# The first of four causal-attention chunks computed with its keys down the partitions, as the other three are

## The reference

```python
xn = layernorm(x)                                   # eps 1e-5
# attention on xn
x_norm = layernorm(xn) * gamma + beta
q, k, v = x_norm @ qkv[:, :512], x_norm @ qkv[:, 512:1024], x_norm @ qkv[:, 1024:]
scores = where(causal, (q @ k.T) / sqrt(512), -inf)
attn = softmax(scores) @ v @ o_proj + xn
# feed-forward on xn
h = silu(xn @ w_gate) * (xn @ w_up)                 # 2048 x 2048
h = the two of each group of 4 that are largest by magnitude, the others 0
return x + attn + h @ w_down
```

## Time and profile before

| | |
|---|---|
| median of 3 runs | 789.93 us (789.58 to 789.95) |
| the profiled execution | 789.84 us |
| its span, first to last instruction | 788.0 us |
| PE busy | 783.7 us, 99% of the span, 3518 matmuls |
| DVE busy | 610.8 us, 78% |
| ACT busy | 318.9 us, 40% |
| POOL busy | 16.7 us, 2% |
| DMA | 121.74 MB, mean 154 GB/s |

### The profile page before, as it was taken

One profiled execution on the slowest core, in us unless ns is written; L12 is line 12 of the kernel. 1 busy time (PEld: TensorE's weight loads), 2 busy tenths in 40 slices (PEclk: granted clock), 3 DMA queues, 4 the chain that ended last, 5 costly groups with the idle time before them and its releaser, 6 DMA issues.

```text
span 788.0 us, 9292 instructions
## 1 busy us (share of the span) xinstructions
PE 783.7 (99%) x3518; PEld 649.1 (82%) x3518; DVE 610.8 (78%) x964; ACT 318.9 (40%) x514; POOL 16.7 (2%) x26
## 2 busy tenths in 40 slices
PE   9999999999999999999999999999999999999998
PEld 6888878888888888888888888888888888888887
DVE  6988788678535797789989789798658658659786
ACT  5432250235123473464643634463423424335431
POOL 2011110010000000000000000000000000000000
PEclk9999999999999999999999999999999999999999
DMA  9541704500121643684454352697277163161002
GB/s 317 190 161 55 241 0 163 192 20 1 54 94 40 214 172 122 199 343 179 187 211 181 143 189 106 269 355 284 79 280 260 48 240 126 62 240 54 0 1 107
DMA packets 31611, 121.74 MB, mean 154 GB/s; under 512 B 3088, under 2 KB 3664, under 8 KB 29136
## 3 DMA queue, kind: packets, MB, share of 16 engines
q1 hardware_dynamic: 30272, 119.00, 40.9%
q10 hardware_dynamic: 1296, 2.16, 0.9%
HBM read 77.07 MB, written 44.07 MB: 154 GB/s over the span
## 4 chain that ended last, share of the span: by engine, by line
PE 98%; DMA 1%; SPq 0%; ACT 0%; DVE 0%; issue 0%
PE bank L960 13%; PE bank L958 13%; PE bank L959 13%; PE bank L701 10%; PE bank L699 10%; PE bank L700 10%; PE bank L1038 7%; PE bank L838 7%; PE bank L1040 7%; PE bank L1039 7%; DMA raw<-L_attn_qkv 1%; SPq L483 0%; PE bank L709 0%; PE bank L804 0%; PE bank L771 0%; PE bank L1051 0%
## 5 line engine op out<-in xcount | busy, mean ns | idle before, releaser
L958 PE MATMUL bank<-X_hi,wset 128*128 128x512 f32 x448 | 174.6, 390 | 0.0
L959 PE MATMUL bank<-X_lo,wset 128*128 128x512 f32 x448 | 174.5, 389 | 0.0
L960 PE MATMUL bank<-X_hi,wset 128*128 128x512 f32 x448 | 174.5, 389 | 0.0
L960 PEld LDWEIGHTS bank<-X_hi,wset 128*128 128x128 f32 x448 | 84.1, 188 | 17.5
L959 PEld LDWEIGHTS bank<-X_lo,wset 128*128 128x128 f32 x448 | 84.1, 188 | 17.5
L958 PEld LDWEIGHTS bank<-X_hi,wset 128*128 128x128 f32 x448 | 84.1, 188 | 17.3 <-issue 0.2
L1038 PE MATMUL bank<-dw,hs_hi 128*128 128x512 f32 x224 | 87.3, 390 | 0.0
L1039 PE MATMUL bank<-dw,hs_hi 128*128 128x512 f32 x224 | 87.2, 389 | 0.0
L1040 PE MATMUL bank<-dw,hs_lo 128*128 128x512 f32 x224 | 87.2, 389 | 0.0
L1672 DVE TENSOR_TENSOR acc<-bank,acc 128x512 f32<-128x512 f32 x59 | 40.2, 688 | 40.0 <-PE bank L1040 39.6
L699 PE MATMUL bank<-zg,xT 128*128 128x512 f32 (+2 forms) x132 | 49.9, 378 | 0.0
(11 more groups left out here) (259 smaller groups left out, 1445.3 us busy)
## 6 DMA issues: line engine op xcount, KB each, us to landing
w_operands<-wset SPq DMA_DIRECT2D x8, 3584.0 KB, 13.2
wset<-w_operands SPq DMA_DIRECT2D x8, 3584.0 KB, 12.2
wsum<-w_units SPq DMA_DIRECT2D x28, 256.0 KB, 3.4
dw_raw<-L_ffn_w_down SPq DMA_DIRECT2D x14, 512.0 KB, 5.0
xw<-L_attn_x SPq DMA_DIRECT2D x4, 1024.0 KB, 9.9
xt_raw<-x_t SPq DMA_DIRECT2D x8, 512.0 KB, 9.2
xn_t<-xt_raw SPq DMA_DIRECT2D x8, 512.0 KB, 2.8
acc<-resid SPq DMA_DIRECT2D x2, 2048.0 KB, 10.1
```

The source lines that it names most:

```text
L958: pe.matmul(dst[:], u[:, 0, :], x_hi, start=(first and kt == 0), stop=False, skip_group_check=True)
L959: pe.matmul(dst[:], u[:, 0, :], x_lo, start=False, stop=False, skip_group_check=True)
L960: last = pe.matmul(dst[:], u[:, 1, :], x_hi, start=False, stop=(kt == 1), skip_group_check=True)
```

## The change

Chunk 0 is made wide too: `WIDE = range(NCH)`. The kinds `scores`, `exp`, `head` and `attend` and the ring of transposed exponentials go. Chunk 0 has four units, all on the diagonal, and three parts for the softmax: unit 0, unit 1, units 2 and 3 together. Its maximum goes into one tile instead of a pair (no `max_fold`), its sums too (`first_sums`). The stretch between the products z(0) and the second chunk is written anew; all row steps of chunk 0 come into the stretch of chunk 1, and their stores and loads go to SP's queue; `row_turn(2)` comes behind the first unit of chunk 1. Units go round the banks from where the products stand (`unit_bank`), and the transposes of statistics for chunks 2 and 3 take bank 2 (`row_bank`). The matrix `causal` for the other orientation is no longer made.

```diff
-    steps += [*vo, *stat[1][0:2], *z[0], *stat[1][2:4], x_stats[1], x_rstd[1], xw_load[3], v[0][0],
-              ("scores", 0, 0), exp[0], x_scale[1], row_copy[1], v[0][1], row_turn[1], row_store[1], row_spread[1]]
-    before = {3: [z_round[1][0]]}
-    between = {3: [*stat[2][2:4], x_stats[2], x_rstd[2], *z_round[1][1:4], *z[1], x_scale[2]]}
-    beside = {0: [*stat[2][0:2], v[0][2]],
-              1: [xh_pre[1][0], v[0][3], xh[1][0]],
-              2: [xh_pre[1][1], xh_pre[1][2], xh[1][1], xh_pre[1][3], xh[1][2], xh[1][3]]}
-
-    WIDE = (1, 2, 3)
-    OLD = TC * WIDE[0]
-    for i in range(OLD):
-        steps += before.get(i, [])
-        steps.append(("head", i, 0))
-        if i >= 1:
-            steps.append(("rows_store", i - 1, 0))
-        steps += between.get(i, [])
-        if i + 1 < OLD:
-            steps += [("scores", i + 1, 0), exp[i + 1]]
-        steps += [*beside.get(i, []), ("attend", i, 0), ("rows", i, 0), ("rows_load", i + 1, 0)]
+
+    WIDE = range(NCH)
 
     def wide_units(c):
...
+    u = unit[0]
+    steps += [v[0][0], *u[0:2], x_scale[1], *u[2:4], ("max_all", 0, 0), row_turn[1], row_copy[1], row_store[1], row_spread[1], v[0][1]]
+    steps += softmax(0, {1: [v[0][2]], 2: [v[0][3]]}, {})
+    steps += [xh_pre[1][0], *meet[0][0:2]]
+    steps += [step for k in range(KT) for step in (*xh_pre[1][k + 1:k + 2], xh[1][k], z_round[1][k])]
+    steps += [*stat[2], x_stats[2], x_rstd[2], meet[0][2], *z[1], x_scale[2], ("sum_turn", 0, 0)]
     u = unit[1]
-    steps += [row_turn[2], row_copy[2], row_store[2], row_spread[2], *u[0:2], ("rows_store", OLD - 1, 0), *xn[1], xt_load[2], xn_store[1],
-              *stat[3], x_stats[3], x_rstd[3], xt_load[3], *u[2:4], x_scale[3], u[4], row_turn[3], row_copy[3], row_store[3], xh_pre[2][0], u[5],
-              xh_pre[2][1], xh[2][0], u[6], xh_pre[2][2], xh[2][1], u[7], ("max_fold", 1, 0), ("max_all", 1, 0), ("rows_load", OLD + 1, 0),
+    steps += [u[0], row_turn[2], row_copy[2], row_store[2], *rows_of[0][0], *rows_of[0][1], row_spread[2], ("rows_load", 2, 0), ("rows_load", 3, 0),
+              u[1], *xn[1], xt_load[2], xn_store[1], *stat[3], x_stats[3], x_rstd[3], xt_load[3], *rows_of[0][2], *rows_of[0][3],
+              ("rows_load", 4, 0), ("rows_load", 5, 0), *u[2:4], x_scale[3], u[4], row_turn[3], row_copy[3], row_store[3], xh_pre[2][0], u[5],
+              xh_pre[2][1], xh[2][0], u[6], xh_pre[2][2], xh[2][1], u[7], ("max_fold", 1, 0), ("max_all", 1, 0),
               xh_pre[2][3], xh[2][2], v[1][0], xh[2][3], *v[1][1:4], *z_round[2]]
     steps += softmax(1, {}, {2: [*z[2], *xn[0], xn_store[0]], 4: [("block_sum", 0, 0)]})
-    steps += [("sum_turn", 1, 0), row_spread[3], *rows_of[1][0], *rows_of[1][1], ("rows_load", OLD + 2, 0), ("rows_load", OLD + 3, 0)]
+    steps += [("sum_turn", 1, 0), row_spread[3], *rows_of[1][0], *rows_of[1][1], ("rows_load", 6, 0), ("rows_load", 7, 0)]
...
-                elif kind == "rows_store" and n >= OLD:
+                elif kind == "rows_store":
                     sp.wait_ge(rows_ready, n + 1)
                     sp.dma_start(resid_dram[n], row_slot(n)).then_inc(resid_stored[n % 2], 16)
-                elif kind == "rows_load" and OLD + 2 <= n < NT - 2:
+                elif kind == "rows_load" and n < NT - 2:
                     load_rows(n)
...
-            nc.gpsimd.memset(causal[:], 0.0).then_inc(pool_step, 1)
...
-            def score_product(n, g):
-                t, count = score_spans(n)[g]
-                no, a = prod_no["scores", n, g], n % TC * P
-                if n == 0:
...
-                if no >= TURN_RING:
-                    pe.wait_ge(turn_free, no - TURN_RING + 1)
-                row_bank_free(no)
+                if n == 1:
+                    pe.wait_ge(prod_free, 2 * KT)
+                elif n == 3:
+                    pe.wait_ge(wide_kept, units_ahead[1] + LENT_BANK + 1)
                 pe.wait_ge(scale_ready, n + 1)
...
-            def turn_probs(n, g):
-                no = turn_no["probs", n, g]
...
-                for b, t in enumerate(key_tiles(n)[g]):
-                    last = pe.transpose(dst_bank[:, b * P:(b + 1) * P], raw[:, n % 2, t * P:(t + 1) * P], ident[:])
-                last.then_inc(turn_full, 1)
...
-                    pe.wait_ge(prod_free, prods_before[c])
-                    if c > WIDE[0] and u == SUM_BANK:
-                        pe.wait_ge(sums_read, c - WIDE[0])
+                    pe.wait_ge(prod_free, max(prod_no["z", c, KT - 1] + 1, prods_before[c] - PROD_RING + u + 1))
+                    if c > 0 and u == SUM_BANK:
+                        pe.wait_ge(sums_read, c)
                 else:
                     pe.wait_ge(wide_kept, seen + u - PROD_RING + 1)
+                if c == 1 and u % PROD_RING == LENT_BANK:
+                    pe.wait_ge(turn_free, 2 + u // PROD_RING)
...
                 for m in range(KT):
                     if n == WIDE[-1] and q == 0:
                         pe.wait_ge(wide_kept, units_ahead[n] - PROD_RING + 1 + m)
+                    elif n == 1 and q == m == 0:
+                        pe.wait_ge(wide_kept, units_ahead[n])
...
                 elif kind == "v":
                     pe.wait_ge(prod_free, prod_no["vo_weight", 0, KT - 1] + 1)
                     pe.wait_ge(xh_ready, KT * (n + 1))
-                    if n in (WIDE[0], WIDE[-1]):
+                    if n == 0 and k:
+                        pe.wait_ge(wide_kept, k)
+                    elif n in (1, WIDE[-1]):
                         pe.wait_ge(wide_kept, units_ahead[n] + len(wide_units(n)) - PROD_RING + 1 + k)
                     product(kind, n, k, (xT_hi[n], xT_lo[n]), k * P, (vo_hi, vo_lo))
-                elif kind == "scores":
-                    pe.wait_ge(prod_free, prod_no["z", n // TC, KT - 1] + 1)
-                    for g in range(len(score_spans(n))):
-                        score_product(n, g)
-                elif kind == "head":
-                    turn_head(n)
-...
                 masked = step(nc.vector.tensor_tensor(block[:, 0:P], block[:, 0:P], causal_t[:], ALU.add))
                 dve.wait_ge(vec_step, masked)
-                wide_done[c] = step(nc.vector.tensor_tensor(half[:, u % 2, a:W], half[:, u % 2, a:W], block, ALU.max))
+                if c:
+                    wide_done[c] = step(nc.vector.tensor_tensor(half[:, u % 2, a:W], half[:, u % 2, a:W], block, ALU.max))
+                    return
+                one = max_one[0][:, a:W]
+                if u == 0:
+                    wide_done[c] = step(nc.vector.tensor_copy(one, block))
+                    return
+                dve.wait_ge(vec_step, wide_done[c])
+                largest_yet = nc.vector.tensor_tensor(one, one, block, ALU.max)
+                if u < TC - 1:
+                    wide_done[c] = step(largest_yet)
+                else:
+                    largest_yet.then_inc(max_folded, 1)
 
...
+            def first_sums(j):
+
+                dve.wait_ge(exp_made, j + 1)
+                whole = sum_pair[0][:, 0, :]
+                if j == 0:
+                    sums_done[0] = step(nc.vector.tensor_copy(whole, raw_part(0, 0)))
+                    return
+                for u in wide_parts(0)[j]:
+                    some = whole[:, unit_cols(0, u):W]
+                    dve.wait_ge(vec_step, sums_done[0])
+                    added_up = nc.vector.tensor_tensor(some, some, raw_unit(0, u), ALU.add)
+                    if u < TC - 1:
+                        sums_done[0] = step(added_up)
+                    else:
+                        added_up.then_inc(sums_ready, 1)
+
             def add_part(c, j):
 
                 sums, units = sum_pair[c], wide_parts(c)[j]
+                if c == 0:
+                    first_sums(j)
+                    return
                 dve.wait_ge(exp_made, parts_ahead[c] + j + 1)
                 if j < 2:
```

More of the change, by code:

```diff
@@ L67, in attention_ffn @@
     xn = [fills("xn", c)[0:2] for c in range(NCH)]
-    exp = [("exp", n, 0) for n in range(NT)]
     hi, lo = ([fills(kind, m) for m in range(4)] for kind in ("split_hi", "split_lo"))
@@ L134, in attention_ffn @@
     steps += softmax(2, {-1: [z[3][2]], 0: [z[3][3]], 1: v[2][0:2], 2: v[2][2:4]}, {4: [xn[3][0]], 5: [xn[3][1], xn_store[3]]})
-    steps += [("sum_turn", 2, 0), *rows_of[2][0], ("rows_load", OLD + 6, 0), *rows_of[2][1], ("rows_load", OLD + 7, 0)]
+    steps += [("sum_turn", 2, 0), *rows_of[2][0], ("rows_load", 10, 0), *rows_of[2][1], ("rows_load", 11, 0)]
     u = unit[3]
@@ L140, in attention_ffn @@
     w_hi_steps, w_lo_steps = fills("w_hi", 0), fills("w_lo", 0)
-    steps += [*u[0:4], *rows_of[2][2], ("rows_load", OLD + 8, 0), *rows_of[2][3], ("rows_load", OLD + 9, 0), *u[4:6], ("w_sum", 0, 0), u[6],
+    steps += [*u[0:4], *rows_of[2][2], ("rows_load", 12, 0), *rows_of[2][3], ("rows_load", 13, 0), *u[4:6], ("w_sum", 0, 0), u[6],
               *w_hi_steps[0:2], *u[7:9], *w_lo_steps[0:2], *u[9:], ("max_fold", 3, 0),
@@ L147, in attention_ffn @@
```

(36 more changed lines are left out.)

150 lines of the change are left out of this document (34 added, 116 removed).

## The result

| | before | after |
|---|---|---|
| median | 789.75 us (789.55 to 789.95, 4 runs) | 795.54 us (795.19 to 796.23, 4 runs) |
| the profiled execution | 789.84 us | 795.4 us |
| its span | 788.0 us | 793.4 us |

What follows compares the result with a forecast made beforehand. TensorE was taken as the bound, issuing back to back at full clock, so any wait adds to the total. The terms -0.66 + 0.75 + 1.0 + 3.8 = +4.9 us on 789.84 gave 794.7 us, range 792.6 to 797.0.

Steps and rivals of the forecast that it cites:

- The transposes: On TensorE in chunk 0, ten transposes of the exponentials go and four of the column sums come: minus 0.66 us.
- The wait of z_round(1, 0): After chunk 0's softmax, PE waits for xT_hi(1, 0), late behind a long VectorE queue: 0.7 to 0.8 us, taken as 0.75.
- GpSimd's code: Before GpSimd's first all-reduce, a code fetch of 7.5 us outlasts the 6.0 us gap, making the first shift 1.0 us late.
- Rival 1: The all-reduce's code is there in time, so that term is nothing: 793.7 us; chance 0.22.
- The sign that the prediction named for it: GpSimd's gap before the first all-reduce: 6.0 if no code is fetched, more with "issue" as cause if it is.
- The wait of row_turn(3): In chunk 1, VectorE's queue from row_turn(2) takes 14.8 us against PE's 11.05, so PE waits 3.8 us; the largest term.
- The claim that idle time is wholly used up: VectorE's 3.02 us of idling for unit 3, ahead of x_scale(3), is counted as used up in its queue's sum.
- The wait of the earlier trace: PE's existing 0.5 us wait at 107.07, hanging on PE's own v(1, 3), its cast and its subtraction, stays.
- 4 (half the wait): Row_turn(3) waits only half as long, some row steps overlapping, and GpSimd's code is in time: about 791.9 us; chance 0.07.
- 3 (faster): VectorE finishes in time, PE never waits, for instance with row_turn(2) before unit 0; only transposes count: 789.2 us; chance 0.04.

Runs made afterwards that it cites:

- the probe: The changed kernel with one small GpSimd memset, waiting for unit 2 of chunk 0, put ahead of the first all-reduce; 800.0 us in one execution.

## Why the prediction was right

The forecast was 794.7 us in a range of 792.6 to 797.0, slower with 0.93; it is 795.54. Step by step:

- **The transposes, -0.66 us.** The last matmul ahead of z_round(1, 0) starts at 61.83, so PE would have issued the next at 62.06; forecast 62.25. Until row_turn(3) the rows leave -0.70 for the transposes (0.14 behind, less 0.89 for the wait below, and this execution starts its scores 0.05 sooner). Right.
- **The wait of z_round(1, 0), +0.75.** 0.74 by the profile, 0.89 by the starts (62.95 - 62.06), in the place and for the tile that was named; the forecast had PE start there at 62.95. Right.
- **GpSimd's code, +1.0.** It is 0. A gap of 5.72 us is real (the probe), but it fits into the 6.18. The term was sized by the nearest row, 8.84 at the program's start; why that one is longer is open. Rival 1 was the case. The sign that the prediction named for it (a gap of 6.0 if no code is fetched) could not have told a fetch that fits from none; it took the probe.
- **The wait of row_turn(3), +3.8.** 3.72 by the profile, 3.88 by the starts. Each of VectorE's starts between 79.48 and 93.79 fell where the sum has it, within 0.05 us: 14.8 us less 11.05. That the queue is the cause was shown by row_turn(2) moved ahead: 2.1 us sooner in, 2.0 us less wait. The claim that idle time is wholly used up was right. That the sum names no other limit near was an omission: with 2.6 us taken out, GpSimd's chain left 0.3 us of it to win.
- **Missing: the clock, +1.38.** The prediction forecast a standstill of 3.8 us and put what the clock does behind it at nothing. No row of the kernel before shows a fall. Filling the wait with work brought the time down by 1.5 us.
- **The wait of the earlier trace rows, unchanged.** Right: 1.56 us from the first matmul of z_round(2, 0) to the one that waits, in both kernels.

With the terms as measured: -0.05 - 0.70 + 0.89 + 0 + 3.88 + 1.38 = 5.40, the difference of the spans. The mechanism of the largest term was forecast and is shown; that the total came within 1 us is partly luck, because two errors, 1.0 too much for the code and 1.4 too little for the clock, have opposite signs. Of the rivals, 4 (half the wait) and 3 (faster) are out; 3's remark that row_turn(2) ahead of unit 0 would help was worth 3.3 us, though not the whole.

## What to carry to other kernels

When a tensor engine is busy all the time, add up the queue of the engine beside it between two points where they meet, idle time included; what the sum has over is the wait, here to 0.1 us. Before moving work off such a queue look for the limit just under it (here a chain through a third engine, 0.3 us away) and for the next point where the backlog is met: three of the moves only carried the wait elsewhere. Compare starts of the same instructions in both kernels and not the idle times in brackets: 0.7 for 0.5 was no loss at all, and 0.74 was 0.89. And see where a copy or a scale waits for a tiny transpose behind a long unit: that one move was worth more than the change could gain.

## What was not expected of the hardware

- The granted clock fell from 1.00 to 0.50 at the end of standstills of 3.72 us (changed kernel) and 3.37 us (row steps in the softmax), but not at one of 3.37 us (row steps behind row_turn(3)), where it fell at 112.0 us, behind waits of 0.21 and 0.70. It also fell with no standstill over 1.9 us: at waits of 1.86 and 0.70 (row_turn(3) behind the last unit), and at 67.4 us in the probe, behind waits of 1.42 and 1.80. It did not after 1.72 or 1.65. So the length of one standstill did not tell whether it would fall. It came back after some 3 us in the changed kernel and over 6 in two others (row steps in the softmax, row_turn(3) behind the last unit).
- GpSimd went from an elementwise operation to the all-reduce in 5.72 us with nothing else between. From the memsets to the first select it takes 8.24 us in the changed kernel.
- The first of GpSimd's two `radicand` operations, 128x4, took 1.11 us when VectorE had just begun a maximum of 128x1024, 0.43 beside a row step in the changed kernel, and 0.23 at 42.31 there.
